# Pair products from triangles of points, with block input in two buffers

## What is computed

```python
m = x.shape[1]                       # 39
x0 = x; xk = x; outs = []
for W in (W0, W1):
    Hk, Hn = xk.shape[1], W.shape[-1]        # 39 then 128; 128
    Wr = W.reshape(m, Hk, Hn)
    xk = jnp.einsum('bid,bjd,ijh->bhd', x0, xk, Wr)
    outs.append(xk)
return jnp.sum(jnp.concatenate(outs, axis=1), axis=-1)
```

## Time and profile before

| | |
|---|---|
| runs | 582.6 us median of 3 (582.31 to 584.89) |
| profiled execution | 579.92 us |
| its span | 578.1 us |
| busy: TensorE, weight loads | 550.1 us (95%), 483.1 us (84%) |
| busy: DVE, ScalarE, GpSimd | 472.1 us, 470.0 us, 480.9 us |
| transfers | 163.78 MB, 283 GB/s on average |

### The profile page before, as it was taken

The page is one execution under the profiler, slowest core; times in us unless marked ns, Lnnn a source line. Parts: engine busy times, 40 slices in busy tenths (PEclk is TensorE's granted clock), DMA queues, the critical chain, the costliest instruction groups (busy, mean ns, idle before and its releaser), DMA issues.

```text
span 578.1 us, 10856 instructions
## 1 busy us (share of the span) xinstructions
PE 550.1 (95%) x3186; PEld 483.1 (84%) x3186; DVE 472.1 (82%) x816; ACT 470.0 (81%) x983; POOL 480.9 (83%) x407
## 2 busy tenths in 40 slices
PE   5788788999999999999999999999999999999998
PEld 3476677878888888988988998898889889889988
DVE  4688888888888898888889888888988888888740
ACT  4698888889888888888888888888888888888740
POOL 6998899899989888889988888898888899888800
PEclk9799999999999999999999999999999999999999
DMA  8999999999899989999999989999999989988210
GB/s 318 331 352 317 326 312 304 306 305 295 267 306 332 307 298 290 279 324 287 288 301 312 303 268 305 315 296 293 313 285 281 325 292 300 295 304 285 52 52 10
DMA packets 66489, 163.78 MB, mean 283 GB/s; under 512 B 10112, under 2 KB 18816, under 8 KB 66432
## 3 DMA queue, kind: packets, MB, share of 16 engines
q1 hardware_dynamic: 66432, 163.09, 88.0%
HBM read 139.98 MB, written 2.10 MB: 246 GB/s over the span
## 4 chain that ended last, share of the span: by engine, by line
PE 71%; ACT 10%; DMA 6%; issue 5%; POOL 4%; DVE 2%; SPq 1%; ACTq 0%; DVEq 0%; POOLq 0%
PE acc L397 12%; PE acc L399 11%; PE acc L398 11%; PE fin L448 6%; PE fin L449 6%; PE fin L450 6%; DMA outs<-w_dram 5%; PE pg L433 5%; PE pg L431 5%; PE pg L432 5%; ACT fh L510 4%; PE turn L409 4%; PE acc L392 2%; POOL fl L761 2%; ACT gh L552 1%
## 5 line engine op out<-in xcount | busy, mean ns | idle before, releaser
L761 POOL TENSOR_TENSOR fl<-fs,fh 128x512 fp32r<-128x512 f32 x192 | 249.7, 1304 | 42.8 <-ACT fh L510 40.1
L397 PE MATMUL acc<-fh,w0h 128*128 128x512 f32 x384 | 160.3, 417 | 15.3 <-ACT x L533 10.1
L756 POOL TENSOR_TENSOR fs<-xr,xs 128x512 f32<-128x512 f32 x128 | 163.0, 1295 | 0.9 <-DMA xr<-xb_dram 0.8
L647 DVE TENSOR_TENSOR fp<-xl,xr 128x512 f32<-128x512 f32 x192 | 133.5, 697 | 31.4 <-ACT xl L517 18.4
L399 PE MATMUL acc<-fl,w0h 128*128 128x512 f32 x384 | 151.9, 395 | 0.0
L398 PE MATMUL acc<-fh,w0l 128*128 128x512 f32 x384 | 151.5, 395 | 0.0
L651 DVE TENSOR_TENSOR fl<-fp,fh 128x512 fp32r<-128x512 f32 x192 | 131.9, 687 | 23.1 <-ACT fh L510 18.2
L510 ACT ACTIVATE fh<-fp 128x512 fp32r<-128x512 f32 x192 | 114.5, 596 | 36.3 <-PE acc L399 30.6
L666 DVE TENSOR_TENSOR gl<-pg,gh 128x320 fp32r<-128x320 f32 x252 | 117.0, 486 | 25.8 <-ACT gh L552 20.6
L510 ACT ACTIVATE fh<-fs 128x512 fp32r<-128x512 f32 x192 | 121.4, 632 | 10.8 <-PE acc L399 8.6
L552 ACT ACTIVATE gh<-pg 128x320 fp32r<-128x320 f32 x252 | 105.5, 439 | 18.4 <-PE pg L433 17.6
(11 more groups left out here) (67 smaller groups left out, 724.0 us busy)
## 6 DMA issues: line engine op xcount, KB each, us to landing
xr<-xb_dram SPq DMA_DIRECT2D x192, 512.0 KB, 5.7
xbd<-xdhl SPq DMA_DIRECT2D x256, 80.0 KB, 4.0
xs<-xa_dram SPq DMA_DIRECT2D x64, 256.0 KB, 4.1
xdr<-xd_dram SPq DMA_DIRECT2D x64, 160.0 KB, 3.9
xp<-xpairs_dram SPq DMA_DIRECT2D x32, 256.0 KB, 4.3
outs<-w_dram SPq DMA_DIRECT2D x9, 256.0 KB, 6.6
out_dram<-outs SPq DMA_DIRECT2D x7, 256.0 KB, 5.8
fs<-w0a_dram SPq DMA_DIRECT2D x1, 256.0 KB, 4.8
```

The lines of the kernel that those rows point to most:

```text
L397: nc.tensor.matmul(acc[:, :], w0h[:, t, :], fh[:, t, :], start=t == 0, stop=False)
L647: nc.vector.tensor_tensor(f_at(t), xl[:, :], xr[:, gi % 2, t, :], ALU.mult).then_inc(prod_dve, 1)
L756: nc.gpsimd.tensor_tensor(f_at(t), xr[:, gi % 2, t, :], xs[:, gi % 2, :], ALU.mult)\
L761: nc.gpsimd.tensor_tensor(fl[:, t, :], f_at(t), fh[:, t, :], ALU.subtract).then_inc(low_pool, 1)
```

## The change

Each of 128 partitions now holds a triangle of points (a, b, c) instead of one left point. The left operand is a. Right places 0 and 1 hold b and c; tile 0 is a x b, tile 2 is a x c, and tile 1 is b x c, a product of two right operands. Tiles 3, 4 and 5 are a with three more points, as before. So five right blocks serve six tiles. They come in three transfers: places 0 and 1, places 2 and 3, and place 4 alone. Which pairs stand where is worked out on the host (`triples`, `labels`, `pair_slots`), and W0's rows are placed accordingly.

The block input `xdr` has two buffers, with a semaphore each; SP loads that of group g+3 in the round of group g, at the end of the round, behind the right operands. The pieces of W1 have a buffer of their own, `w1r`, which also takes the first weights' second part at the start. `first_out` stands in round 13 for the first chunk.

```diff
+PLACE = {0: 0, 2: 1, 3: 2, 4: 3, 5: 4}
+BOTH_RIGHT = 1
+NR = len(PLACE)
+PARTS = (slice(0, 2), slice(2, 4), slice(4, 5))
+PART_OF = {0: 0, BOTH_RIGHT: 0, 2: 0, 3: 1, 4: 1, 5: 2}
...
+def pair_slots(of):
+
+    for m, row in enumerate(of.tolist()):
+        for t, k in PLACE.items():
+            yield t, m, row[0], row[1 + k]
+        yield BOTH_RIGHT, m, row[1 + PLACE[0]], row[1 + PLACE[2]]
...
-        xr = sb("xr", [P, 2, NT, GC])
+        xr = sb("xr", [P, 2, NR, GC])
...
-        xdr = sb("xdr", [P, 2, NQ, MI])
+        xdr = sb("xdr", [P, 2, 2, NQ, MI])
+        w1r = sb("w1r", [P, NW, H])
...
-                sp.dma_start(xr[:, gi % 2, 2 * u:2 * u + 2, :], xb[CB * j + gi][:, 2 * u:2 * u + 2, :])\
+                sp.dma_start(xr[:, gi % 2, PARTS[u], :], xb[CB * j + gi][:, PARTS[u], :])\
                   .then_inc(xr_in[u][gi % 2], 16)
...
-                sp.dma_start(xdr[:, :, :, :], xd[g]).then_inc(xd_in, 16)
+                sp.dma_start(xdr[:, g % 2, :, :, :], xd[g]).then_inc(xd_in[g % 2], 16)
...
                 if p:
                     sp.wait_ge(w1_ready, p)
                     sp.wait_ge(w1_ready_dve, p)
+                else:
+                    sp.wait_ge(w0_ready, 3)
...
                     if more3:
-                        wait_product(sp, g + 1, 0)
                         wait_product(sp, g + 1, 4)
+                        wait_product(sp, g + 1, 2)
                         load_x(j, gi + 3)
                         load_right(j, gi + 3, 0)
                     blocks(g, gi, first)
...
-                    if not (last and gi + 1 >= CB):
-                        sp.wait_ge(xd_low, g + 2)
-                    if more2:
-                        load_xd(g + 2)
                     if more3:
                         wait_product(sp, g + 1, 3)
                         load_right(j, gi + 3, 1)
                     if more3:
                         wait_product(sp, g + 1, 5)
                         load_right(j, gi + 3, 2)
+                    if not (last and gi + 1 >= CB):
+                        sp.wait_ge(xd_low, g + 2)
+                    if more3:
+                        load_xd(g + 3)
                     if (first or second) and 0 <= g + 1 - W1_SLOT < PIECES:
                         w1_load(g + 1 - W1_SLOT)
...
-                if t == POOL_PROD[0]:
+                if t == BOTH_RIGHT:
+                    left, place = xr[:, gi % 2, PLACE[0], :], PLACE[2]
+                else:
                     pool.wait_ge(xs_in[gi % 2], 16 * nth(j, gi))
-                pool.wait_ge(xr_in[t // 2][gi % 2], 16 * nth(j, gi))
+                    left, place = xs[:, gi % 2, :], PLACE[t]
+                pool.wait_ge(xr_in[PART_OF[t]][gi % 2], 16 * nth(j, gi))
...
-                if c == 0:
-                    pool.wait_ge(w1_ready, PIECES)
-                    pool.wait_ge(w1_ready_dve, PIECES)
...
-                    if gi == (CB - 1 if second else 5) and not first:
+                    if gi == 5 and not first:
                         first_out(j - 1, not odd)
```

More of the change, by code:

```diff
@@ L21 @@
 TILES = NT + 1
-LOADED = range(NT)
+HALF = M // 3
+PLACE = {0: 0, 2: 1, 3: 2, 4: 3, 5: 4}
[3 more added lines that the diff above has]
+PART_OF = {0: 0, BOTH_RIGHT: 0, 2: 0, 3: 1, 4: 1, 5: 2}
+STARS = (3, 4, 5)
 LEFT = range(18, 30)
@@ L44 @@
 HIGH = (0, 1, 2, 4, 3, 5)
-NU = NT // 2
+NU = len(PARTS)
 W0_PART = 4
@@ L70, in pieces_before, with triples, point, labels @@
     return min(-(-row // NW), PIECES)
[L73 to L79, removed]
+def triples():
+    def point(x, i):
+        return HALF * (i % 3) + x % HALF
+    yield from ((point(x, 0), point(x, 1), point(x, 2)) for x in range(HALF))
+    for x in range(HALF):
+        for y in range(x + 1, HALF):
+            for i in range(3):
+                yield point(x, i), point(y, i), point((x + y) * (HALF + 1) // 2, i + 1)
+def labels():
+    system = list(triples())
+    whole = {k * len(system) // P for k in range(P)}
+    count = [0] * M
+    rows = []
+    for triple in (system[k] for k in sorted(whole)):
+        apex = min(triple, key=lambda v: (count[v], v))
+        count[apex] += 1
+        rows.append((apex, *(v for v in triple if v != apex)))
+    pairs = [(t[k], t[l]) for n, t in enumerate(system) if n not in whole
+             for k, l in ((0, 1), (0, 2), (1, 2))]
+    pairs += [(i, i) for i in range(M) if i not in LEFT]
+    cap = [len(STARS) * c for c in count]
+    held = {v: [] for v in range(M)}
     def settle(pair, tried):
@@ L98, in pair_slots @@
         assert settle(pair, set())
-    free = {v: [(t, m) for t in LOADED for m in range(v, P, M)] for v in cap}
-    return [(*free[v].pop(), v, i + j - v) for v, got in held.items() for i, j in sorted(got)]
+    out = []
+    for apex, b, c in rows:
+        out.append((apex, b, c, *(sum(held[apex].pop()) - apex for _ in STARS)))
+    return np.array(out)
+def pair_slots(of):
[3 more added lines that the diff above has]
+        yield BOTH_RIGHT, m, row[1 + PLACE[0]], row[1 + PLACE[2]]
 def left_rows(u):
@@ L152, in build @@
         w0a_raw = [fs[:, SBUF_F[4], :].rearrange("p (t h) -> p t h", h=H),
-                   xr[:, 1, NT - 1, :].rearrange("p (t h) -> p t h", h=H)]
+                   w1r[:, :, :]]
         w0b_raw = [outs_as_w, x1[:, :].rearrange("p (t h) -> p t h", h=H)]
@@ L170, in build @@
         sq_ready = sem("sq_ready")
-        xd_in = sem("xd_in")
+        xd_in = [sem("xd_in0"), sem("xd_in1")]
         xd_high = sem("xd_high")
@@ L201, in w1_raw @@
         def w1_raw(p):
-            rows = outs[:, :, :].rearrange("p a b -> p (a b)").rearrange("p (n h) -> p n h", h=H)
-            return rows[:, 0:piece(p).stop - piece(p).start, :]
+            return w1r[:, 0:piece(p).stop - piece(p).start, :]
         def tile_n(g, t):
@@ L355, in _ @@
             load_right(0, 1, 0)
+            load_right(0, 1, 1)
+            load_right(0, 1, 2)
             load_xd(0)
-            load_right(0, 1, 1)
             sp.dma_start(idn[:, :], ident).then_inc(ident_in, 16)
-            sp.wait_ge(w0_ready, 3)
-            load_right(0, 1, 2)
-            wait_product(sp, 0, 0)
+            load_xd(1)
             wait_product(sp, 0, 4)
+            wait_product(sp, 0, 2)
             load_x(0, 2)
             load_right(0, 2, 0)
-            sp.wait_ge(xd_low, 1)
-            load_xd(1)
             wait_product(sp, 0, 3)
@@ L370, in _ @@
             load_right(0, 2, 2)
+            sp.wait_ge(xd_low, 1)
+            load_xd(2)
             chunk(0, True, False, False)
@@ L536, in xd_split @@
                 g = CB * j + gi
-                act.wait_ge(xd_in, 16 * (g + 1))
+                act.wait_ge(xd_in[gi % 2], 16 * nth(j, gi))
                 if not fresh:
                     act.wait_ge(xbd_in[gi % 2], 16 * (BQ // 2) * (nth(j, gi) - 1))
-                nc.scalar.activation(xdhl[:, gi % 2, :, :, 0, :], xdr[:, :, :, :], COPY).then_inc(xd_high, 1)
+                nc.scalar.activation(xdhl[:, gi % 2, :, :, 0, :], xdr[:, gi % 2, :, :, :], COPY).then_inc(xd_high, 1)
             def turned_high(g):
@@ L642, in product @@
                     dve.wait_ge(xl_ready, g + 1)
-                dve.wait_ge(xr_in[t // 2][gi % 2], 16 * nth(j, gi))
+                dve.wait_ge(xr_in[PART_OF[t]][gi % 2], 16 * nth(j, gi))
                 dg, dt = BEFORE_IN_F.get(t, (-1, t))
@@ L646, in product @@
                     wait_low(dve, g + dg, dt)
-                nc.vector.tensor_tensor(f_at(t), xl[:, :], xr[:, gi % 2, t, :], ALU.mult).then_inc(prod_dve, 1)
+                nc.vector.tensor_tensor(f_at(t), xl[:, :], xr[:, gi % 2, PLACE[t], :], ALU.mult).then_inc(prod_dve, 1)
             def low(g, t):
@@ L750, in product @@
                 g = CB * j + gi
-                if t == POOL_PROD[0]:
+                if t == BOTH_RIGHT:
+                    left, place = xr[:, gi % 2, PLACE[0], :], PLACE[2]
+                else:
                     pool.wait_ge(xs_in[gi % 2], 16 * nth(j, gi))
-                pool.wait_ge(xr_in[t // 2][gi % 2], 16 * nth(j, gi))
+                    left, place = xs[:, gi % 2, :], PLACE[t]
+                pool.wait_ge(xr_in[PART_OF[t]][gi % 2], 16 * nth(j, gi))
                 if not fresh:
                     wait_low(pool, g - 1, t)
-                nc.gpsimd.tensor_tensor(f_at(t), xr[:, gi % 2, t, :], xs[:, gi % 2, :], ALU.mult)\
-                  .then_inc(prod_pool, 1)
+                nc.gpsimd.tensor_tensor(f_at(t), xr[:, gi % 2, place, :], left, ALU.mult).then_inc(prod_pool, 1)
             def low(g, t):
@@ L827 @@
     xt = x.transpose(1, 0, 2).reshape(M, NG, GC)
-    xa = np.ascontiguousarray(xt[np.arange(P) % M].transpose(1, 0, 2))
+    of = labels()
+    xa = np.ascontiguousarray(xt[of[:, 0]].transpose(1, 0, 2))
     rows = [*PICKED, *LEFT]
@@ L840 @@
     xd = xd.reshape(NG, P, 2, NQ, MI)
-    right = np.zeros((FULL, P), np.int64)
     w0a = np.zeros((P, len(ORDER), H), w0.dtype)
     w0b = np.zeros((P, len(ORDER), H), w0.dtype)
```

(5 more changed lines are left out.)

2 lines of the change are left out of this document (1 added, 1 removed).

## The result

The change makes the kernel **faster**, by three quarters of a per cent: 576.36 us, the median of 15 runs (574.44 to 578.92), against 581.96 us for the kernel before, the median of 15. The ratio is 0.9925, with a 95% interval of 0.9903 to 0.9947. The forecast was 577.5 us.

A forecast was written before the change was run, and what follows sets the result against it. TensorE was taken as full from 160 us on, leaving only its 22.6 us of idle time before 152 us. Profiled 579.92 - 4.0 (piece waits) - 1.1 (start) = 574.8; off the 582.6 median, 577.5 us, range 574.5 to 581.5.

The forecast's parts named there:

- The ring of the pieces: Rounds 6 to 15: ScalarE's seven waits for second-weights pieces, 6.41 us, mostly go; worth 4.0 us.
- the bound of 4.92: Rounds 6 to 15: most that removing every wait for a piece could gain, 89.67 us down to 84.75.
- The rival in which the landing doesn't move: Pieces still land in 6.6 us, all seven waits stay, only the start gains: 581.5 us; chance 0.18.
- The landing: Rounds loading a weights' piece: 256 KB less ahead brings it 0.85 us sooner, bounds 0 and 1.9.
- The rows 6.1 and 4.2: Landing times in us of a 512 KB right piece and a 256 KB left block, giving the 1.9 us bound.
- The floor: Rounds 6 to 15 without piece waits: five at 8.64, one at 7.95, four at 8.40, together 84.75 us.
- The start: Rounds 0 and 1: a second block-input buffer removes two ScalarE waits; worth 1.1 us, between 0.39 and 2.78.
- The two waits of the earlier trace: ScalarE's split waiting for the block input, 1.24 us in round 0 and 1.54 in round 1; both to go.
- SP's start: First block input goes out behind 512 KB more; taken as no cost, up to 1.6 us kept for a rival.
- the slow rival: Late first block input lengthens TensorE's pause, clock stays low past 30 us: 6.2 us more, 583.7 us; chance 0.08.
- The rest: Other parts, such as the product of two right operands and loads waiting for DVE's tile 2: worth nothing.
- The second stage's ring: 30 to 62 us: ScalarE's copy x1 and TensorE wait on each other, so fewer bytes are worth nothing.

The follow-up runs named there:

- e2: The changed kernel with 256 KB more per round, read by nobody, ahead of the weights' piece, `first_out` back in round 15: 580.72 us, ratio 0.9996.
- e5: The kernel before, all its bytes kept, only the weights' piece issued ahead of the second and third right transfers: 576.8 us, ratio 0.9947.
- e11: The changed kernel with 256 KB unread per round issued behind the weights' piece, `first_out` back in round 15: 579.02 us, ratio 0.9960.
- e4: The changed kernel with the first block input issued ahead of group 1's second and third right transfers: 577.6 us, ratio 0.9938.
- e7: The changed kernel with weights' pieces in two buffers, loaded a round earlier, first block input moved ahead, first output sum in round 15: 577.09 us, ratio 0.9937.
- e10: The kernel of e7 with added matmuls of constants, result unused, in TensorE's pauses of rounds 0 to 5: 576.4 us, ratio 0.9914.
- e3: The changed kernel with 256 KB more per round, read by nobody, in the 45 rounds from round 16 on: 576.02 us, ratio 0.9914.
- e1: The changed kernel with the block input in one buffer, loaded for group g+2 at the end of SP's round: 580.29 us, ratio 0.9983.
- after_again: The changed kernel run and profiled once more, nothing altered (its second profile): 577.18 us, ratio 0.9936.
- e9: The kernel of e4 with 27 added matmuls of constants, result unused, in TensorE's pauses of rounds 0 to 5: 576.42 us, ratio 0.9931.

## Why the prediction was right

**The ring of the pieces: right.** The term was 4.0 us, and the rounds gave 4.27; they were to take 85.7 us and took 85.40; 1.18 us of waits were to be left and 1.03 were. e2 gives the gain back by the bytes ahead of the piece, and e5 gets it by the place alone. That the size fits so closely is luck in part: in the second profile no wait is left and the rounds gave 89.67 - 84.67 = 5.00 us, just over the bound of 4.92. The rival in which the landing doesn't move falls with the landing.

**The landing: mis-sized.** The term took 0.85 us off the landing, with an upper bound of 1.9; measured are 6.6 - 4.4 = 2.2 us by the medians, outside the bounds, and 1.7 and 1.9 us by the means of the two profiles (table above), twice the term. The rows 6.1 and 4.2 that made the bound compare two places in one full queue, and sizes of 512 and 256 KB besides. With 256 KB less in every round the whole queue drained sooner: the left operand, which has the same bytes ahead of it in its burst, gained 1.4 us by itself. That part was missing; that the rest, 0.8 us, is the bytes just ahead is only arithmetic, and e11's 4.7 us with all the bytes back doesn't fit it well. The Trainium skill's fit ("DMA: Bandwidth & Descriptors", "Anatomy of one DMA": about 2 us that no size changes, and bytes at 436 GB/s) gave 0.60 us, an estimate from the page; the 2.2 us measured here disagree, by more than my own figure does.

Why did the sum hold all the same? Errors met. The piece is issued 0.4 us later in its round on the mean, which the prediction had at nothing, so that it lands 1.3 us sooner in its round, not 2.2. Even so all seven waits of the earlier trace rows, none longer than 1.28, should have gone, and in the second profile they did; in the first, one of 1.03 us stayed, since landings scatter, and that piece took 6.68 us in the chain that ended last:

```profile
121.25 6.68 DMA w1r<-w_dram
```

**The floor: right as a sum, wrong in its parts.** 84.75 us were forecast, and e4, e7 and e10 measure 84.68 to 84.71. But the odd rounds were not held at 8.40, nor the others at 8.64: behind the first four, e4's rounds last 8.93 and 8.10 us by turns, and the two errors cancel, which is luck.

**The start: mis-sized.** Forecast 1.1 us, measured 0.40. The two waits of the earlier trace rows went, as said. The prediction took no cost for SP's start, and that step was wrong in the first profile: the first split waits 0.55 us and stands at 16.58 instead of 15.52 us, the mechanism that I had kept for the slow rival at up to 1.6 us. In the second profile it does not wait, and x1 of round 2 comes at 29.46 us, 1.02 before the 30.48 of the kernel before. But e11's split waits 0.30 us with x1 at 30.06, and e3's 0.27 with x1 at 29.43, so this wait alone doesn't set the 0.6 us between the two; what does stays open. The clock fell past 30 us in one of the two profiles of the changed kernel, as that rival had it, but not by that wait, which is absent from that very execution; x1 of round 6 came 2.4 us later for it, not 6.2.

**The rest: right.** The second stage's ring and the middle's 8.40 us are unmoved, though DVE's tile 2 now stands ahead of every load; e3 shows that the bytes are worth nothing there.

The sum on the profiled execution was 574.8 us; it came to 575.58. The gain was forecast as 5.1 us; it is 4.3 us between the profiled executions and 5.6 between the medians.

## What to carry to other kernels

Before bytes are cut, look at which transfer ends a wait and where it stands in its queue: here moving one issue past two others was worth nearly as much as cutting a sixth of the right operands, and the bytes saved in the 45 rounds without a piece bought nothing. Read when in its round a transfer lands, and not only how long it took. When a load moves to the end of a round, look whether its buffer is free early enough there: with one buffer, e1 waited 3.09 us for it. And profile the same program twice before a difference of 2 us in one profile is given a cause.

## What the runs showed of the hardware

I had not expected that TensorE's clock falls in some executions of a program and not in others. The places were 38 to 44 us (after_again, e2, e3), 70 to 76 (e11), 32 to 38 and 90 to 96 (e1), 82 to 88 (e2) and, in e9, this one, from its busy times by stretch; below it the same part of the same round in the changed kernel's first profile, where nothing fell:

```profile
84.00:88.00 4.00, 2.54 (x13) 1.68 (x11) 3.87 (x8) 4.00 (x10) 3.76 (x5) 1.00 1.00 287
88.00:92.00 4.00, 3.94 (x13) 3.36 (x14) 3.20 (x6) 1.53 (x5) 3.73 (x4) 0.57 0.86 309
```

```profile
83.67:87.67 4.00, 2.54 (x12) 1.66 (x11) 3.87 (x8) 4.00 (x10) 3.93 (x5) 1.00 1.05 325
87.67:91.67 4.00, 3.94 (x21) 3.44 (x22) 3.61 (x8) 3.08 (x9) 4.00 (x5) 1.00 0.82 299
```

In e9 TensorE is busy 2.54 of 4 us, and then the granted clock averages 0.57, near the lower level of 1.2 GHz, for 4 us; it gets through 13 matmuls instead of 21. In the changed kernel it is busy the same 2.54 of 4 us, and the clock stays at 1.00. The round's code and the pause before are alike in both, so the rows do not say why the clock falls in one of them. e9's round took 10.03 us, against 8.46. By the lengths of their rounds such falls cost 1.6 us (e9, e11, e1) to 2.2 us (after_again, 9.97 against 7.81), against the 4.5 us over which the first 15 runs of the changed kernel spread; whether falls make that spread, only the profiled executions could show. With the pauses of rounds 0 to 5 filled (e9) the spread was 2.7 us; twelve runs don't show whether that is the reason.
